# Graph attention on one core: each head's source logits come to the partitions by DMA and no longer by matmuls of scaled identities

## The reference, cut to what matters

```
hv = h.reshape(n, H, DIN)                       # 1250 x 12 x 64
ft = jnp.einsum('nhd,od->nho', hv, W)
a1 = jnp.sum(ft * attn_l, axis=-1)              # source logits, 1250 x 12
a2 = jnp.sum(ft * attn_r, axis=-1)              # target logits
e = jax.nn.leaky_relu(a1[src] + a2[dst], negative_slope=NEG_SLOPE)
w = jnp.exp(e - m[dst])                         # m: maximum over a target's edges
alpha = w / jnp.maximum(denom[dst], 1e-16)      # denom: sum of w over a target's edges
agg = jax.ops.segment_sum(alpha[:, :, None] * ft[src], dst, num_segments=n)
out = jax.nn.relu((agg + res).reshape(n, H * DOUT))   # res: hv through W_res
```

## Time and profile before

| | us |
|---|---|
| median of 3 runs | 3424.27 |
| lowest and highest of the runs | 3413.43, 3425.73 |
| the profiled execution: its time | 3441.28 |
| the profiled execution: its span, first to last instruction | 3439.5 |
| mean granted clock of TensorE in it | 0.957 of full |

### The profile page before, as it was taken

The page is one execution under the profiler, slowest core; times in us unless marked ns, Lnnn a source line. Parts: engine busy times, 40 slices in busy tenths (PEclk is TensorE's granted clock), DMA queues, the critical chain, the costliest instruction groups (busy, mean ns, idle before and its releaser), DMA issues. The chain is left out here.

```text
span 3439.5 us, 61775 instructions
## 1 busy us (share of the span) xinstructions
PE 3240.6 (94%) x20813; PEld 3025.1 (88%) x20813; DVE 2173.2 (63%) x4034; ACT 1335.0 (39%) x2527; POOL 922.2 (27%) x968
## 2 busy tenths in 40 slices
PE   6998989999998999999999999999989797899998
PEld 6886778888888999999988999999979495799998
DVE  7898456766777520137878401258868454499998
ACT  1344232333323111124446311134555211388885
POOL 1104534444554310014456200034456000000000
PEclk9999999999999999999999999999999797699997
DMA  3134353423213343347867533367767203000001
GB/s 81 46 105 139 97 137 83 101 50 100 61 31 92 109 142 100 102 157 242 242 207 235 171 111 101 101 203 242 238 204 228 92 1 76 12 1 0 0 0 46
DMA packets 164966, 386.06 MB, mean 112 GB/s; under 512 B 34418, under 2 KB 103583, under 8 KB 164758
## 3 DMA queue, kind: packets, MB, share of 16 engines
q0 software_dynamic: 47200, 173.39, 16.9%
q1 hardware_dynamic: 80074, 147.20, 15.2%
q10 hardware_dynamic: 37484, 62.75, 6.0%
HBM read 283.93 MB, written 99.32 MB: 111 GB/s over the span
## 5 line engine op out<-in xcount | busy, mean ns | idle before, releaser
L1877 PE MATMUL bank<-w_hi,xT_hi 128*125 128x384 f32 x1920 | 650.4, 339 | 0.0
L1878 PE MATMUL bank<-w_lo,xT_hi 128*125 128x384 f32 x1920 | 648.6, 338 | 0.0
L1879 PE MATMUL bank<-w_hi,xT_lo 128*125 128x384 f32 x1920 | 648.5, 338 | 0.0
L1563 ACT COPY arena<-bank 125x384 f32<-125x384 f32 x320 | 153.7, 480 | 793.2 <-PE bank L1879 762.5
L830 POOL DMA_INDIRECT arena<-y_early,edges x204 | 229.4, 1125 | 821.5 <-DMA y_late<-arena 320.4
L904 DVE SCALAR_TENSOR_TENSOR row_lo<-arena,edges,row_hi 128x768 fp32r<-128x768 f32 x300 | 304.2, 1014 | 124.4 <-ACT row_hi L873 84.1
L2345 DVE CAST w_hi<-w_raw 128x2304 fp32r<-128x2304 f32 x35 | 47.6, 1360 | 517.8 <-PE bank L1879 512.5
L1878 PEld LDWEIGHTS bank<-w_lo,xT_hi 128*125 128x125 f32 x1920 | 356.5, 186 | 0.1
L1877 PEld LDWEIGHTS bank<-w_hi,xT_hi 128*125 128x125 f32 x1920 | 356.5, 186 | 0.0
L1879 PEld LDWEIGHTS bank<-w_hi,xT_lo 128*125 128x125 f32 x1920 | 356.3, 186 | 0.1
L743 ACT ACTIVATE arena<-arena,low 125x1250 f32<-125x1250 f32 x170 | 227.7, 1339 | 327.7 <-DVE low L755 327.7
(11 more groups left out here) (359 smaller groups left out, 6685.7 us busy)
## 6 DMA issues: line engine op xcount, KB each, us to landing
y_early<-arena SPq DMA_DIRECT2D x200, 180.0 KB
w_raw<-in_L_gnn_W_dram ACTq DMA_DIRECT2D x30, 1152.0 KB, 6.4
arena<-own_mask_d SPq DMA_DIRECT2D x50, 585.9 KB
y_late<-arena SPq DMA_DIRECT2D x120, 180.0 KB
h_d<-arena ACTq DMA_DIRECT2D x40, 250.0 KB
arena<-in_L_gnn_W_dram SPq DMA_DIRECT2D x5, 1536.0 KB, 10.8
arena<-h_d ACTq DMA_DIRECT2D x30, 250.0 KB
wadj_d<-arena SPq DMA_DIRECT2D x10, 625.0 KB
```

The source lines that it names most:

```text
L1877: pe.matmul(b, xT_hi[:, k, v], w_hi[:, h, k], start=(k == 0), stop=False)
L1878: pe.matmul(b, xT_hi[:, k, v], w_lo[:, h, k], start=False, stop=False)
L1879: ins = pe.matmul(b, xT_lo[:, k, v], w_hi[:, h, k], start=False, stop=(k == KD - 1))
```

## The change

All 12 columns of source logits are turned at once: 12 transposes on PE into banks 0 to 2, and six copies with the sign turned on ACT into `alT3` (heads 0, 2, 4, ... in its first half, which lies in `iota_row`, and 1, 3, 5, ... in its second). SP stores both halves into a DRAM tensor `s_d`, 12 x 1250. Head 0's row is spread on PE from `alT3` by ten matmuls, whose stationary operand is a column of the identity repeated 125 times, and copied by `act_spread` as before. For the heads 1 to 11 SP loads the row of `s_d` to all 125 partitions in two transfers (120 and 5 partitions); from head 2 on it waits until the last unit of head h - 2 is masked. ACT makes the sloped copy in one instruction in its step 4. The scaled identities on DVE, the spreading matmuls in the loop on PE, and ACT's copies from the banks in steps 3 to 5 are gone.

```diff
-        def dve_diag(dve, v, ring, sd, als):
-
-            dve.wait_ge(s_spread, unit(v - ring))
-            dve.tensor_scalar(sd, ident[0:P, 0:P], als, -1.0, op0=ALU.mult, op1=ALU.mult).then_inc(diag_made, 1)
-
-        def pe_spread(pe, v, t, b0, sd):
-            pe.wait_ge(diag_made, v + (1 - V3))
-            pe.matmul(bank[b0 + t // 4][0:P, (t % 4) * P:(t % 4 + 1) * P], ones[0:P, 0:P], sd, start=True, stop=True).then_inc(s_spread, 1)
+        def pe_spread(pe, t, q, i, b0):
+            pe.matmul(bank[b0 + t // 4][0:P, (t % 4) * P:(t % 4 + 1) * P], ident[0:NT, t:t + 1].to_broadcast([NT, P]),
+                      alT3[q][:, bass.ds(i, 1)].rearrange("p o n -> p (o n)"), start=True, stop=True).then_inc(s_spread, 1)
...
+            sp.wait_ge(al_ready, H0 + 4)
+            for q in range(2):
+                sp.dma_start(s_d.rearrange("(i q) (t n) -> q t i n", q=2, n=P)[q], alT3[q]).then_inc(s_stored, 16)
+            sp.wait_ge(s_stored, 32)
+            for h in range(1, H3):
+                if h >= 2:
+                    sp.wait_ge(score_masked, unit(V3 + (h - 1) * NT - 1))
+                for lo, hi in ROWS:
+                    sp.dma_start(s_row3[lo:hi, h % 2], spread(s_d[h], hi - lo)).then_inc(s_row_loaded[h % 2], 16)
...
             for c in range(3):
+                act.wait_ge(al_turned, H0 + 2 + c)
+                for q in range(2):
+                    ins = act.activation(alT3[q][:, 2 * c:2 * c + 2], bank[c][0:NT, 0:4 * P].rearrange("p (i q n) -> p i q n", q=2, n=P)[:, :, q], ACT.Copy, scale=-1.0)
+                ins.then_inc(al_ready, 1)
+            for c in range(3):
                 ins = act_spread(act, V3, c, 5, s_row3[:, 0], s_low3[:, 0])
             ins.then_inc(s_row_ready, 1)
...
-                    if 3 <= d < 6 and (q == 1 or not last):
-
-                        ins = act_spread(act, u + q * NT, d - 3, 5, s_row3[:, q % 2], s_low3[:, q % 2])
-                        if d == 5:
-                            ins.then_inc(s_row_ready, 1)
+                    if d == 4 and (q == 1 or not last):
+                        act.wait_ge(s_row_loaded[q % 2], 32 * (i + 1))
+                        act.activation(s_low3[:, q % 2], s_row3[:, q % 2], ACT.Copy, scale=SLOPE).then_inc(s_row_ready, 1)
...
+            for h in range(H3):
+                ins = pe.transpose(bank[h // 4][0:NT, h % 4 * P:(h % 4 + 1) * P], al3[:, 0, :, h], ident[0:P, 0:P])
+                if h % 4 == 3:
+                    ins.then_inc(al_turned, 1)
+            pe.wait_ge(al_ready, H0 + 2)
             for t in range(NT):
-                pe_spread(pe, V3 + t, t, 5, s_diag3[:, t % 4])
+                pe_spread(pe, t, 0, 0, 5)
+            pe.wait_ge(al_ready, H0 + 4)
...
-                    if d < NT // 2 and (q == 0 or not last):
-                        if d == 0:
-                            pe.wait_ge(s_row_ready, h + (H0 + 2))
-                        for t in (2 * d, 2 * d + 1):
-                            pe_spread(pe, u + ((q + 1) * NT + t), t, 5, s_diag3[:, ((q + 1) * NT + t) % 4])
...
-            for t in range(NT):
-                diag_3(V3 + t, t, 0, t)
...
                     def between():
-                        then = rden_3(u + (k + 1), k + 1) if k + 1 < PAIR or not last else None
-                        if d < NT // 2 and (q == 0 or not last):
-
-                            for t in (2 * d, 2 * d + 1):
-                                n = (q + 1) * NT + t
-                                diag_3(u + n, n, i * 2 + (q + 1), t)
-                        return then
+                        return rden_3(u + (k + 1), k + 1) if k + 1 < PAIR or not last else None
```

More of the change, by code:

```diff
@@ L359, in build @@
         s_low3 = cut(rest + NT * N + node + 2 * NT * H3 + 2 * N, 2, N, parts=P)
-        s_diag3 = cut(rest + NT * N + node + 2 * NT * H3 + 4 * N, 4, P + 3, parts=P)[:, :, 0:P]
+        alT3 = [iota_row[0:NT, 0:H3 // 2 * P].rearrange("p (i n) -> p i n", n=P),
+                cut(rest + NT * N + node + 2 * NT * H3 + 4 * N, H3 // 2, P, parts=NT)]
+        assert NT * N + node + 2 * NT * H3 + 4 * N + H3 // 2 * P <= REST
         s_row_low = iota_row[0:P, 0:N]
@@ L401, in build @@
         x_d = dram("x_d", [N, D])
+        s_d = dram("s_d", [H3, N])
         wadj_d = dram("wadj_d", [NT, P, NT * CT])
@@ L427, in build @@
         h_made, h_ready = sem("h_made"), sem("h_ready")
-        diag_made, s_spread, s_row_ready = sem("diag_made"), sem("s_spread"), sem("s_row_ready")
+        s_spread, s_row_ready = sem("s_spread"), sem("s_row_ready")
+        s_stored, s_row_loaded = sem("s_stored"), [sem(f"s_row_loaded{i}") for i in range(2)]
         w3_cleared, w3_loaded, w3_turned, w3T_ready = sem("w3_cleared"), sem("w3_loaded"), sem("w3_turned"), sem("w3T_ready")
@@ L2501, in _ @@
             chain(dve.tensor_scalar(al3[:, 1], al3[:, 1], SLOPE - 1.0, None, op0=ALU.mult))
-            def diag_3(v, k, h, t):
-                dve_diag(dve, v, 4, s_diag3[:, k % 4], al3[:, 0, t, bass.ds(h, 1)])
             def mask_3(v, m, h, between=None):
```

## The result

Twenty runs of each kernel, on the same chip, give a median of 3399.89 us for the changed kernel (3391.77 to 3422.93) and 3413.90 us for the kernel before (3406.46 to 3436.56). The ratio is 0.9953, with a 95% interval of 0.9939 to 0.9968: of 3413.9 us that is 16.0 us less, 10.9 to 20.8. (The two medians are 14.0 us apart.) The change makes the kernel faster by an amount that is just under half a per cent and clear of no change. The forecast was 12.2 us less, and "within 0.5%" as what a measurement could not tell from no change. The forecast time, 3412, lies 12.1 us above the result, and 10.4 of these are the level from which the 12.2 were taken: the three runs shown ahead had a median of 3424.27, where twenty have 3413.90.

The account below looks back on a forecast made before the run. PE was taken to bound the kernel, DVE 2% behind and the bound after the change. Loop -13.0, pause +0.3 and entry +0.5 gave -12.2 us, from the median 3424.27 to 3412; range 3399 to 3425.

Parts of the forecast that it names:

- within 0.5%: Whole kernel: the outcome class of a change too small to tell from none, about 17 us; chance 0.74.
- main term: Loop, DVE's units 4 to 113: 109 steps fall from 381.22 us to 368.2 at 3.378 each, gain 13.0 us.
- the entry's chain: Entry, turning logits on PE and six ACT copies: head 0's copies end 0.5 us later, bounds -0.3 and 2.5.
- Its clock: Entry: if PE is at half clock there, its matmuls double and the entry's cost reaches 2.5 us.
- The pause of 0.31 us at the mask of unit 6: Code-loading pause at 3006.80 that may stay hidden no longer: cost 0.3 us, at most 1.5 over five loop passes.
- A row: Loop transfers: a 610 KB row lands in 14 us, bounds 7.4 and 30, with 23.6 us available; no cost.
- the slack of PE's sums: Loop: PE delivers each sum 1.5 us ahead of DVE's need, so DVE runs at 3.378 without waiting.
- A: Loop: PE's removal counts in full, 24.0 us less 0.8 at the ends, giving 3401; chance 0.08.
- B: Loop, PE in steady state: the clock falls, one step in ten at half costs 38 us, giving 3450; chance 0.06.
- The rule of the Trainium skill: Loop clock: transposes would not help hold it, only sums of 2.13 us a step; the forecast sum was left standing.
- C: Loop: rows come late, at 30 us instead of 14 ACT waits 6.4 us in ten heads, giving 3461; chance 0.02.
- D: Loop: small stalls covered by PE's slower pace come out, 0.5 to 1 us a head, giving 3420; chance 0.14.

Follow-up runs that it names:

- the two repetitions: The changed kernel, unedited, measured twice more against the kernel before, 12 runs each time: ratios 0.9981 and 0.9969.
- PE's work back: Changed kernel with two 125 x 125 matmuls put back on PE in steps 0 to 4 of each head but the last: 3412.64 us, ratio 1.0008 to before.
- DVE's work back: Changed kernel with two scaled identities put back on DVE in steps 0 to 4 of each head but the last: 3420.19 us, ratio 1.0008 to before.
- the kernel with the sum in the gap: Changed kernel with DVE taking the previous unit's sum between the reciprocal's two instructions, until the last head: 3393.66 us, ratio 0.9895 to before.
- the late rows: Changed kernel with each row's transfer released five masks later, heads 2 to 11: 3397.38 us, ratio 0.9922 to before, steps of 3.375 us.

## Why the prediction was right and wrong

The step that failed is "A measurement of this kernel can tell from no change about 0.5%, 17 us. The forecast is 12, or 0.36%: within", and with it the 0.74 put on "within". Twenty runs of each kernel told 0.47% with an interval of 0.3% to 0.6%, a half-width of 5 us and not 17, so the forecast of 12 us should have been called a gain. Twelve runs are at the edge: the two repetitions have intervals that reach 1.0003 and 0.9998. The forecast gives no working for the 17 us.

The step beside it is "I take the 12.2 from the median". The median was that of three runs of a kernel whose runs spread over 30 us, and it stood 10.4 above that of twenty. The range was to allow for this with "some room" and held the result by 0.9 us only, which was luck.

The mechanism was right. PE set the pace before (PE's work back: the gain is gone). DVE sets it after, at 3.375 a step against 3.378 read ahead (DVE's work back: 3.51 a step). The sum, 12.2, agrees with the 12.6 of all runs and with the 11.7 of the profiles' networks, and lies in the interval of the first comparison.

Its main term was a little too large. From unit 4 to 113, priced at 13.0 us, it is 381.22 us before and 368.89 after in the first profiles, 12.3: the first of these steps took 4.38 us with PE at half clock, where 3.378 was put. From unit 5 to 113, without that step, it is 13.0 (377.53 and 364.51).

The terms beside the loop: the entry's chain was put at 0.5 us and is 0.35 to 0.6. Its clock was put at up to 2.5. The steps to unit 6 took 21.6 and 24.5 us before and 23.0 after three times, so with two profiles of before no cost of the change is shown there. The pause of 0.31 us at the mask of unit 6, put at 0.3, is in both profiles of before and in none of after; that it comes from the loading of code is the forecast's reading and no run tests it. A row was put at 14 us to land and takes 4; the slack of PE's sums, put at 1.5, is about 1.2 (a sum that ends at 3141.42 is taken at 3142.58) and was never used up in the loop.

Of the rivals, A (24 us) was wrong for the reason given, and the kernel with the sum in the gap shows what it lacked. B did not occur: the clock stood at 1.00 from unit 6 to unit 113. The rule of the Trainium skill weighed there, that transposes do not count as PE-busy in the way other matmuls do ("TensorE: Matmul & The Clock Gate", Part 4: PE-mode transpose), cost nothing here: with a third of PE's time in transposes and no spreading matmuls at all, the loop ran at full. Whether the sums alone held the clock, as the rule would have it, no run tells. C is refuted by the late rows. D did not occur: no odd long step in 108.

One thing stays open: the first comparison has 16.0 us where the network has 11.7 in the mean of the profiles. All runs together have 12.6, and both intervals hold 12.2, so chance is enough. But that the stage ahead is at half clock less often with the change is not excluded: both profiles of before have it, four of the eleven with the change, and none of the three of the changed kernel unedited. Its instructions are the same.

## What to carry to other kernels

Before pricing what is taken from the busiest engine, read the second engine's step in a place where it waits for nobody: the gain ends there, and here that was half of the removed work. Removing work from both engines can be worth more than the sum of the two: here 4.1 us and nothing alone, 12.3 together. A gain that ends so can be had in full by filling a wait in the second engine's own sequence with an independent instruction, while removing an instruction from beside the wait leaves the wait. And when the forecast is smaller than the scatter between runs, the base needs as many runs as the result, or cuts of the trace that the scatter does not touch.

## What the runs showed of the hardware that was not expected

- TensorE stayed at half clock for 36 us and more with matmuls back to back (2940 to 2976, busy 36.00 of 36, granted 0.50), in some executions only, and the same instructions ran at 1.00 in others: 120 matmul records took 72.45 us in one and 39.03 in another.
- A load of one DRAM row of 5 KB to 125 partitions took 4 us from issue to the end of its traffic, at some 200 GB/s, where a row of 3 KB to 125 partitions in another stage took 8.6.
- With a semaphore wait between them, an instruction that needs the result of a 125 x 1 instruction on DVE starts 0.29 us after it, though the first lasts 0.15. One independent instruction, worth 0.20 us of the step elsewhere, stood between at almost no cost: the step fell from 3.375 to 3.18. Two of 0.47 us together cost 0.135.
